# Probabilities turned in 32x32 blocks and put in order by DMA, and a gather that looks two sequences ahead

## The reference, cut to what matters

```python
hidden = concatenate([context, latents])            # 375 + 112 = 487 rows
q = latents @ Wq.T      # 16 heads of 96
k = hidden @ Wk.T       # 4 key heads of 96
v = hidden @ Wv.T
scores = q @ k.T / sqrt(96)                          # 112 x 487 for each of 16 heads
out = softmax(scores) @ v
x = x + tanh(g) * (out @ Wo.T)
```

```python
gathered = take_along_axis(feat, flat_idx)           # layernorm(x): 112 rows x 1024 points
out = einsum('bkm,k->bm', gathered.reshape(8, 16, 1024 * 112), affine_w) + affine_b
```

## Time and profile before

| | |
|---|---|
| median of 3 runs | 3565.14 us (3559.02 to 3574.91) |
| the profiled execution's own time | 3570.34 us |
| its span in the profile | 3568.4 us |
| PE (TensorE) busy | 2993.8 us, 84% |
| DVE (VectorE) busy | 2202.4 us, 62% |
| ACT (ScalarE) busy | 1237.6 us, 35% |
| POOL (GpSimd) busy | 472.4 us, 13% |
| first attention in the span | about 5 to 1037 us |
| gather in the span | about 3050 to 3411 us |

### The profile page before, as it was taken

How to read it: one execution, slowest core, us unless ns; L and a number is a source line. 1 busy time by engine, 2 the same in 40 slices (tenths; PEclk the granted TensorE clock), 3 DMA queues, 4 the chain that set the end, 5 groups by cost and what they waited for, 6 DMA issues and landing times. The chain is left out here.

```text
span 3568.4 us, 58983 instructions
## 1 busy us (share of the span) xinstructions
PE 2993.8 (84%) x21476; PEld 2126.6 (60%) x21476; DVE 2202.4 (62%) x3826; ACT 1237.6 (35%) x2580; POOL 472.4 (13%) x553
## 2 busy tenths in 40 slices
PE   6999999999965999776999999997788786566769
PEld 4665566566543888553655565555777675566634
DVE  4454444544447776555565666664788888698933
ACT  2333333333231333132444444443322332344411
POOL 0110010011022000000222221112222221000000
PEclk9999999999986999887999999998888988788879
DMA  5100110010034554424232233213100000311122
GB/s 217 40 30 11 40 35 24 21 40 30 5 94 166 144 151 137 140 95 178 73 100 103 107 117 117 100 41 132 50 22 17 17 27 16 99 55 54 48 78 62
DMA packets 94345, 270.77 MB, mean 76 GB/s; under 512 B 26264, under 2 KB 48440, under 8 KB 88528
## 3 DMA queue, kind: packets, MB, share of 16 engines
q1 hardware_dynamic: 67216, 162.27, 14.1%
q0 software_dynamic: 22352, 103.44, 8.8%
q10 hardware_dynamic: 4528, 1.84, 0.2%
HBM read 221.31 MB, written 46.19 MB: 75 GB/s over the span
## 5 line engine op out<-in xcount | busy, mean ns | idle before, releaser
L2147 PE MATMUL bank<-ffn_qT,ffn_wgu 128*128 128x112 bf16 x4096 | 244.8, 231 | 58.7 <-DVE ffn_gs L2330 49.5
L2147 PEld LDWEIGHTS bank<-ffn_qT,ffn_wgu 128*128 128x128 fp8e4 x4096 | 240.6, 109 | 64.9 <-issue 62.4
L1600 DVE TENSOR_REDUCE latent_nmax<-bank 112x1 f32<-112x487 f32 x128 | 85.2, 665 | 229.9 <-PE bank L1466 222.4
L2570 PE MATMUL bank<-points_part,points_onehot 128*128 128x56 bf16 x3072 | 121.5, 200 | 95.1 <-DVE points_onehot L2714 94.0
L2277 POOL TENSOR_TENSOR ffn_h<-ffn_sl,ffn_us 128x448 f32<-128x448 f32 x64 | 141.0, 2203 | 400.3 <-ACTq L2232 206.9
L1466 PE MATMUL bank<-latent_kT,latent_wide 96*112 96x487 f32 x256 | 138.1, 634 | 62.2 <-ACTq L1530 59.6
L1427 PEld LDWEIGHTS bank<-latent_hT,latent_wq 128*128 128x128 f32 x1536 | 182.4, 197 | 11.8 <-issue 11.3
L1785 PE MATMUL bank<-grouped_kT,grouped_qT 128*112 128x375 f32 x512 | 179.4, 493 | 6.7 <-ACT grouped_probs L1906 6.7
L2613 ACT ACTIVATE points_spread<-bank 128x512 bf16<-128x512 f32 x256 | 138.7, 593 | 128.1 <-DVE points_onehot L2714 94.5
L1390 POOL TENSOR_SCALAR latent_probs<-latent_probs,latent_rsum 112x487 f32<-112x487 f32 x128 | 88.1, 688 | 716.2 <-DVE latent_rsum L1605 716.2
L1427 PE MATMUL bank<-latent_hT,latent_wq 128*128 128x112 f32 x1536 | 181.0, 279 | 0.0
(11 more groups left out here) (401 smaller groups left out, 6210.4 us busy)
## 6 DMA issues: line engine op xcount, KB each, us to landing
grouped_raw<-L_weights POOLq DMA_DIRECT2D x24, 2048.0 KB, 8.7
codes<-grouped_code SPq DMA_DIRECT2D x24, 512.0 KB, 4.0
latent_hT<-ctxT SPq DMA_DIRECT2D x8, 1500.0 KB, 6.8
plain_ctxT<-ctxT POOLq DMA_DIRECT2D x8, 1500.0 KB, 18.0
plain_ctx<-ctx POOLq DMA_DIRECT2D x8, 1500.0 KB, 35.1
grouped_ctxT<-ctxT SPq DMA_DIRECT2D x8, 1500.0 KB, 11.9
latent_xy<-planes SPq DMA_DIRECT2D x8, 1024.0 KB, 8.4
plain_xy<-planes POOLq DMA_DIRECT2D x8, 1024.0 KB, 9.3
```

The source lines that it names most:

```text
L2147: mm = pe.matmul(ahead.tile(t)[:, i * Q:(i + 1) * Q], wgu[:, u0 + f // 4, c:c + P], qT[:, k, :], start=(k == 0), stop=(k == KC - 1))
L2570: mm = pe.matmul(t_.tile(t)[:, j * AR:(j + 1) * AR], onehot[:, i % 2, j * P:(j + 1) * P], part[n][:, i // K, :], start=(n == 0), stop=(n = ...
```

## The change

In the first attention:
- the keys are cut in tiles of 128, 128, 128 and 103 instead of 125, 125, 125 and 112;
- PE's transposes of the probabilities and VectorE's two copies of each are gone. VectorE transposes the probabilities of a head (padded to 128 x 512) in 32x32 blocks, and for each pair of heads SP stores the blocks to DRAM with 8 DMAs, waits until they have landed, and loads the pair back with one DMA in the order that `outputs` needs;
- scores take four banks instead of two, and `outputs(i)` stands 6 heads behind the scores; `outputs` 5 to 7 stand between and after the projections;
- the squares of tiles 2, 3 and 4 stand after the first and third copy of v and the first copy of k, those of tiles 0 and 1 of the next sequence after the last `outputs` copy;
- the loads of the next context and planes are issued by ScalarE instead of SP.

In the gather:
- the table is cut in blocks of 114 points (9 blocks), 14 partitions are left, and 9 of them hold the block number: one onehot comparison marks both, and a penalty of -2^120 in the table's extra rows makes every block but the right one very negative. Instead of mask, product and sum there is one maximum over 9 blocks, straight out of PSUM;
- the indices are transposed once for a sequence, stored to DRAM and spread to the partitions by DMA (four chunks of 114 and 9 rows of 8 KB), two sequences ahead, in place of PE's spreading and ScalarE's copies;
- x of all 8 sequences stays in SBUF; lookups have three banks, onehots three buffers; nothing is left on GpSimd.

```diff
-    KT = [(k * CT, CT) for k in range(CTILES)] + [(CTX, Q)]
+    KT = [(P * k, min(P, S - P * k)) for k in range(4)]
...
-        order += [(("S", h), 4 + h % 2) for h in range(H)] + [(("pT", h), 6 + h % 2) for h in range(H)]
+        order += [(("S", h), 4 + h % 4) for h in range(H)]
...
             def sequence(p, s, last):
                 b = p * 2 + s
-                if not last:
-                    load_rest(b + 1)
+                for i in range(H // 2):
+                    k, n = i % 2, b * 4 + i // 2
+                    sp.wait_ge(turned, b * H + (2 * i + 2))
+                    if i >= 2:
+                        sp.wait_ge(pT_loaded[k], 16 * n)
+                    for c in range(4):
+                        w = min(32, Q - 32 * c)
+                        for h in range(2):
+                            sp.dma_start(pT_dram[k, :, :, :, h, 32 * c:32 * c + w].rearrange("m k t q -> k t m q"),
+                                         blocks[32 * c:32 * c + 32, k, h * W:(h + 1) * W].rearrange("k (t m q) -> k t m q", t=4, m=4)[:, :, :, 0:w])\
+                              .then_inc(blocks_stored[k], 16)
+                    sp.wait_ge(blocks_stored[k], n * 128 + 128)
...
+                    sp.dma_start(pT[:, k].rearrange("p t h q -> p (t h q)"),
+                                 pT_dram[k].rearrange("m k t h q -> (m k) (t h q)")).then_inc(pT_loaded[k], 16)
...
-                    pe.wait_ge(pT_ready, b * H + (2 * i + 2))
+                    pe.wait_ge(pT_loaded[i % 2], (b * 4 + i // 2) * 16 + 16)
...
+                for h in range(H):
+                    t = ("S", h)
+                    pe.wait_ge(qT_ready, b * 4 + (h // 4 + 1))
+                    pe.wait_ge(turns.free(t), turns.count(t, b))
+                    pe.matmul(turns.tile(t)[0:Q, 0:S], qT[:, h, :], kT[:, h // G, :], start=True, stop=True)\
+                      .then_inc(turns.full(t), 1)
+                    if h >= 6 and h % 2 == 0:
+                        outputs(h // 2 - 3)
+                    if h in (1, 5, 9):
+                        queries(h // 4 + 1)
                 pe.wait_ge(wo_loaded, 16)
                 projected(0)
+                outputs(5)
                 projected(1)
-                outputs(2 * KV - 1)
+                outputs(6)
+                outputs(7)
                 projected(2)
                 projected(3)
...
-                        dve.tensor_copy(pT[0:CT, i % 2, 0:3, h % 2, :], turns.tile(t)[0:CT, 0:3 * Q].rearrange("p (k q) -> p k q", k=3))
-                        dve.tensor_copy(pT[0:Q, i % 2, 3, h % 2, :], turns.tile(t)[0:Q, 3 * Q:4 * Q]).then_inc(turns.free(t), 1)
-                        dve.drain().then_inc(pT_ready, 1)
+                            dve.wait_ge(blocks_stored[k], (b * 4 + i // 2) * 128)
+                        dve.transpose(blocks[:, k, h % 2 * W:(h % 2 + 1) * W], pr[:, h % 3, :]).then_inc(turned, 1)
...
+            def spreading(b):
+                sp.wait_ge(lohi_stored, 16 * b + 16)
+                for c in range(4):
+                    if b >= 1:
+                        sp.wait_ge(onehot_ready, (b - 1) * K + 4 * (c + 1))
+                    for w, r0, n in ((0, 0, CH), (1, CH, NA)):
+                        sp.dma_start(spread[r0:r0 + n, c, :], lohi_dram[b % 3, w, 32 * c:32 * (c + 1), :].rearrange("r c -> (r c)")
+                                     .rearrange("(a n) -> a n", a=1).broadcast_to([n, 4 * D])).then_inc(spread_loaded[c], 16)
+
+            spreading(0)
+            for b in range(1, B):
+                sp.dma_start(x[:, b, :], x_in[b]).then_inc(x_loaded[b], 16)
             early.load(sp)
...
+            for b in range(1, B):
+                spreading(b)
...
+                        mm = pe.matmul(turns.tile(t)[:, j * RA:(j + 1) * RA], onehot[0:ROWS, u % 3, j * P:(j + 1) * P],
+                                       part[n][0:ROWS, b % 2, :], start=(n == 0), stop=(n == 2))
...
+                dve.tensor_reduce(val[:, k].rearrange("p r t -> p t r"), turns.tile(t)[:, 0:KC * RA].rearrange("p (t r a) -> p t r a", t=KC, r=R),
+                                  AX, ALU.max).then_inc(turns.free(t), 1)
+                dve.drain().then_inc(val_ready, 1)
```

More of the change, by code:

```diff
@@ L1370, in sequence @@
                 sp.wait_ge(x_stored[s], p * 16 + 16)
-                if not isinstance(p, int):
+                if p < PAIRS - 1:
                     load_x(b + 2, s)
-            every(sp, sequence)
+            for b in range(B):
+                sequence(b // 2, b % 2, b == B - 1)
             points.stored(sp)
@@ L1594, in sequence @@
                     points.sort(dve, b, 0, i, (5 * s + i) % 2)
[L1595 removed]
+                for step in range(H + 2):
                     h = step
```

579 lines of the change are left out of this document (269 added, 310 removed).

## The result

The changed kernel takes **3668.71 us** (median of 4 runs, 3654.23 to 3676.33), the kernel before 3568.27 us beside it (4 runs, 3559.02 to 3574.91). The ratio is 1.028, with a 95% interval of 1.024 to 1.032: 100 us slower, where 100 us faster was predicted. The two stages went opposite ways, and the first by far more than the forecast's sum had it.

The account below looks back on a forecast made before the run. The prediction held PE to bound the first attention and VectorE the gather, with PE busy 84% overall. From a base of 3565.1 us it took 44 for the attention and 56 for the gather: 3465 us, range 3390 to 3650.

Parts of the forecast that it names:

- 71.3 + 8P: First attention: microseconds per sequence, P being the time from pair to pair; P = 6.2 gives 120.9, -44 over eight.
- start to the first scores: First attention: queries through at 46.6 us, since sorts no longer hold them, plus a 1.6 us copy: 48.2.
- first pair ready: First attention: the first pair of heads is ready for its stores about 5.4 us after the first scores.
- eight pairs, undisturbed (8P - 0.5): First attention: time until the last of eight pairs has its stores landed, at 6.2 us from pair to pair.
- context and planes on the same engines: First attention: 2.5 MB for the next sequence share the DMA engines for 6.3 us; half, 3 us, was counted.
- load of the last pair, then PE's tail: End of a first-attention sequence: load 3.1 us, then one `outputs` (1.6) and two projections (10.5), 12.1 us.
- issues: two took 0.91 us, 0.46 each: First attention, SP: price of issuing a store; the eighth of a pair begins at 3.2 us, ends at 3.7.
- the 0.7 that P was given on top: First attention: microseconds added to a pair's 5.5 for longer patterns and the load on the same engines, giving 6.2.
- Limit of the pieces: First attention rival: 713 pieces a microsecond limit the stores, 8.2 us a pair, +84 us, in all 3593; chance 0.26.
- Slow writes: First attention rival: strided small writes at 26.5 ns a piece, 9.5 us a pair, +167 us, 3676; chance 0.15.
- hidden under 32, barely: Gather: spreading by DMA on six engines takes about 29.5 us a sequence, covered by the 32 us period.
- Gather without gain: Gather rival: six engines can't keep up, period 39, gain about 0, in all 3521; chance 0.08.

Follow-up runs that it names:

- q1_late: Changed kernel with the second query group behind the fourth head instead of the second, on PE and ScalarE: 3612.48 us.
- loads_late: Changed kernel with the next context and planes loaded by SP behind the last pair instead of by ScalarE amid the heads: 3615.61 us.
- two_queues: Changed kernel with four of each pair's eight stores issued by ScalarE and the other four by SP: 3652.09 us.
- early_squares: Kernel before with only the squares of its first attention moved as in the change, plus the changed gather: 3467.54 us, ratio 0.971.
- gather_only: Kernel before with its first attention kept and only the changed gather: 3518.93 us, ratio 0.985.
- late_both: Changed kernel with next context and planes loaded by SP behind the last pair, and the second query group behind the fourth head: 3583.36 us.

## Why the prediction was wrong

**The decision.** The formula for a sequence of the first attention, 71.3 + 8P, had terms in the wrong sizes, and one was missing. The sequence of the profile rows takes 603.55 - 457.58 = 146.0 us against 120.9. Of the 25.1 us:

| term | predicted | measured | difference |
|---|---|---|---|
| start to the first scores | 48.2 | 505.79 - 457.58 = 48.2 | 0.0 |
| first pair ready | 5.4 | 10.7 | +5.3 |
| eight pairs, undisturbed (8P - 0.5) | 49.1 | 6.83 + 7 x 7.40 = 58.6 | +9.5 |
| heads that are late for their pair | none | 1.6 + 2.7 | +4.3 |
| context and planes on the same engines | 3 | 14.19 - 7.40 = 6.8 | +3.8 |
| load of the last pair, then PE's tail | 3.1 + 12.1 | 3.2 + 14.2 | +2.2 |

7.40 is the mean of the four gaps between loads in which nothing else is late; the gaps of 9.03 and 10.09 us give the late heads.

**The step that failed** is the first of the chain's terms, "issues: two took 0.91 us, 0.46 each". A store here takes 0.67. The row was of plain transfers, and two experiments show that the pattern counts and the number of its pieces hardly: 0.44 for eight plain ones, 0.63 with the pattern and a quarter of the pieces. An undisturbed pair is then 5.4 for issuing, 1.5 to landing and 0.4 for the load's issue, 7.3. The landing (1.5 us behind the last issue, for 1.3) was predicted well enough, and the 0.7 that P was given on top is less than half of the 1.7 by which issuing was short. By my own formula P = 7.4 would have given +33 us: enough to turn the sign of this stage, not to make its +150. The other four terms, 15.6 us a sequence, are the second failure, and the larger one: the sum let the first pair, the heads, the loads and PE's clock cost little or nothing beside the chain, and each was paid nearly in full.

**The first pair** was read off the timeline of before as if it were alone, "ready at about 5.4". The second query group and the order of DVE's list were both in the code. `q1_late` gives back 6.7 of the sequence.

**Late heads** were not in the sum at all. PE waits for pair i's load before it goes on to the scores of heads 2i + 7 and 2i + 8, and DVE transposes head h only behind the maximum of head h + 2. So a late load of pair i delays the scores of head 2i + 7, and behind its maximum stands the transpose that completes pair i + 2: the chain feeds itself. On the timeline it is pair 2 that comes late behind pair 0, and pair 5 behind pair 3. This is read from the code and the timeline; no kernel was run without it.

**Contention** was halved to 3 us from the transfer's 6.3 us; it was the whole, 6.8, and `loads_late` gives 7.1 back. The reason, that the chain has no slack in which to hide the other half, is argued.

**PE's clock** I had put at full in the tail. After a wait of 5.7 us the granted clock was 0.50, and the last `outputs` and two projections took 14.2 us instead of 12.1. In this stage PE's one long wait of a sequence in the kernel before is the 7.5 us of the earlier trace rows.

**The rivals.** "Limit of the pieces", P = 8.2, came near in P and is wrong in cause: a quarter of the pieces saves 0.7 us, and `two_queues` moves 1290 packets in a microsecond. "Slow writes" gave 3676, within 8 us of the result, and the trace denies its mechanism: it put a piece at 26.5 ns and a pair's pieces at 7.0 us, and they took 12.5 ns (the last section), 3.3 us a pair, as I had estimated in the sum. That a rival's time fits is no proof of it. The Trainium skill's warning (VectorE: DVE Perf Modes, The three transpose paths) of a factor of 19 for transposes by strides, which the page gives against the crossbar's transpose, did not come true in this form: 128-byte pieces in strided order make a pair 7.4 us where the same bytes in long runs make it 5.3. No run here used the crossbar. The chain through DRAM is expensive by its eight issues and the landing behind them, not by its bytes.

**What held.** The sorts no longer hold the queries (1.6 us before the first scores, as predicted, and 48.2 us from the start of a sequence). VectorE's transpose is 0.69 us. PE's transposes are gone, and that gain, 6.6 us a sequence, is the whole of what the chain could have won; `early_squares` has the other part without it, 119.7 us. The forecast priced the two ideas as one, and so could not say that the one without a transfer was safe.

**The gather** was predicted at -56; it gave -54 in `gather_only` and -36 in the changed kernel's trace. Maximum 0.68 and comparison 0.486 were right. The period, 32.9 for 32, came out right by luck: I had PE as the bound with 28.2 to 33 us a sequence, and in the window of `early_squares` PE is busy 126.63 / 6 = 21.1 us of 32.3 and VectorE 24.3. The pause behind the first sequence was 26.6 and not 13, since I counted the wait for the second spreading alone; it came, 12.8 us, and before it one of 15.7 for x. I also wrote that the chunks on six engines are "hidden under 32, barely". They were not: with the rows cut the period went from 37.9 to 29.3 in the same order on SP, and from 32.3 in the old one. (The Trainium skill, DMA: Bandwidth & Descriptors, Why a DMA increments its semaphore by 16 and not by 1, has the engines as the largest divisor up to 16 of the slowest dimension. From 3300 to 3304 us of the changed kernel, in the spreading of 114 rows, the DMA rows show 73 packets and 38.5% of 16 engines, which is 6 of them; with the cut at 112 rows the share over six sequences is 0.86 instead of 0.51, so the trace agrees.) "Gather without gain" had the cause half right and the size wrong.

**Left open:** what a single store with both mends of `late_both` would take (not run), and so whether a way through DRAM with fewer issues could beat 119.7 us; what the cut of the rows would bring without the new order on SP (not run); what holds the gather at 29.3 us when VectorE needs 24.3; how much of the 0.22 us that the pattern adds to an issue is its dimensions and how much the pieces' number and size (32 of 1792 B in a plain store, 128 or 512 of 128 B in the others). None of them decides here.

## What to carry to other kernels

A chain of issue, landing, issue, landing on one queue is priced by its count of issues and by its distance from the consumer, and each thing that was late in this one, a transfer on the same engines or a consumer that delays the next producer, was paid nearly in full: price an issue from a row with the same kind of pattern, or take a bound well above. When a change bundles several ideas, price and run them apart: moving the squares gained 51 us alone, while the stage that bundled it with the way through DRAM lost 150. And look at the slowest dimension of a transfer: issuing 112 and 2 rows instead of 114 gained 53 us, with nothing else changed.

## What the runs showed of the hardware that was not expected

- A DMA issue on SP took 0.33 us for the load of a pair, 0.44 each in a row of eight plain stores, 0.63 to 0.67 with a pattern of four dimensions, nearly whatever its number of pieces (128 or 512).
- A piece of 128 B kept an engine 12.5 ns, just what I had put between two rows. From 518 to 522 us of the changed kernel only the stores are under way, 3245 packets at 63.4% of 16 engines: 0.634 x 64 us / 3245. The 264 of each engine are then 3.3 us a pair, under the 5.4 of the issues, and so in this kernel they lie beside them.

```profile
q1 hardware_dynamic: 3245, 0.38, 63.4%
```

- SP is held by its own issues when much is under way: seven loads of x took it 20.3 us and one of the weights 13.1, where a plain issue took 0.33 to 0.44 elsewhere. What stood behind them in its list was issued only after.
- The granted clock was 0.50 (1.2 GHz) for the eight multiplications of a pair behind waits of 4.3, 5.7 and 11.7 us, and 1.00 (2.4 GHz) for those behind waits of 0.4, 1.0 and 2.7 us.
